# Attention with distance decay: one product per own chunk, pairs of heads unrolled, far chunks finished on VectorE

## The chip, the cores and the metric

The kernel runs on one core of one Trainium2 chip. The metric is the time of one execution on the device in microseconds (us), the median of several runs. Before the change it is 1452.78 us (three runs, 1446.84 to 1455.47).

A core has a matrix engine (TensorE, PE in the profile, with its weight loads as PEld), VectorE (DVE), ScalarE (ACT), GpSimd (POOL) and SyncE (SP), which here issues the transfers. Each runs its own list of instructions in order, and they wait for one another by semaphores. PSUM is the memory that TensorE writes, here eight banks of 128 partitions by 512 fp32 values; SBUF is the main on-chip memory.

## The reference

For x of shape (2, 2048, 256): layer norm, an attention block, layer norm, add to x; then layer norm, a mixture-of-experts block, layer norm, add. The change is in the attention. Cut to that:

```python
q = x @ W_q;  latent = (x @ W_k + x @ W_v) @ W_down_kv
k_rec = latent @ W_up_k;  v_rec = latent @ W_up_v          # 16 heads of 16 columns
scores = einsum('bhqd,bhkd->bhqk', q, k_rec) / sqrt(256)
decay = exp(-0.01 * abs(t[:, None] - t[None, :]))
attn = softmax(scores * decay)                             # the decay multiplies the scores
out = einsum('bhqk,bhkd->bhqd', attn, v_rec) @ W_o
```

## The kernel before

`prologue` normalises x and makes values, queries and keys of the first unit. `attention` then goes over the 32 heads (16 for each batch) in 16 pairs; `layer` does the rest. In `attention` a head is 16 steps, one for each tile of 128 keys (`kt`), and scores lie with keys on partitions and the 2048 queries along the row, in four chunks of 512.

**The decay.** Queries and keys are stored twice, multiplied by a falling and a rising exponential of their place (`FALL`, `RISE`), so that a product of the two gives a decayed score: RISE is right for queries before the key, FALL for those after it. In the 128x128 block where queries and keys are the same places, FALL is used, and VectorE multiplies the block in PSUM by a mask that mends the half above the diagonal (`mask`, L638). The chunk that holds this block is the tile's own chunk. `score_pieces` (L473) cuts it at the block: RISE before, FALL from it on. Where the block isn't at the chunk's start (12 of 16 tiles) that makes two products of the chunk, so a head has 76 score products (L752).

**Halves and the PSUM ring.** A step's scores are made in two halves of 1024 queries (two banks, one product for each bank, on two halves of TensorE's rows). Six banks make a ring of three halves: the scores of a half wait until the exponential of the half three places earlier is done (`exp_done`). ScalarE takes exp of a whole half, PSUM to SBUF (L841), after the mask where the half holds the own block. The products with the values (L764) of step s-2 stand between the two halves of step s on TensorE's list. They sum in the remaining two banks over a head.

**Far chunks.** For the first and the last four key tiles (`FAR_CHUNK`), the query chunk at the other end of the sequence is so far that exp(z) is taken as ((1 + z)^2 + 1) / 2. VectorE reads it from PSUM as 1 + z into the SBUF tile `probs` (`read_far`, L646); GpSimd squares it (L604) and takes half of it plus a half (L607), both in place; ScalarE leaves this chunk out and its exp for this half is 512 wide. The products of the step wait for GpSimd's last pass (`far_sb`).

**Order.** Every head but the very first takes the key tiles in the order `MIXED` = 4, 0, 5, 1, 6, 2, 7, 3, 8, 12, 9, 13, 10, 14, 11, 15: a near tile, a far tile, and so on. Below, N0 and N1 are the first and second half of a near tile, F0 and F1 those of a far tile. The own block of a near tile is in N0, that of a far tile in F1; the far chunk is in F0. So TensorE's list over two steps runs: scores F1, scores N0, products, scores N1, scores F0, products. VectorE's list over the same two steps: `read_far` of F0, mask of F1, mask of N0.

**What stands between.** VectorE copies a head's sums at step 2 (`copy_sums`, L670), TensorE transposes them at step 4 (L771), VectorE divides at step 5 (`normalise`, L675 and L680, after that step's mask). In the first head of 12 pairs, TensorE projects queries and keys of a later unit at steps 7 and 11 (L726) and VectorE prepares them in three pieces each (`prepare`, L657 to L666) at steps 8 to 10 and 12 to 14, after the mask of the step. Below, these are the prep heads (0, 2, ..., 22). Head 0 runs all tiles in their natural order; head 31, the last, leaves out the far treatment and holds work of the next stage.

**The loop.** `pairs` (L530) writes out pair 0, runs pairs 1 to 9 in a hardware loop of three turns with three pairs in its body, and writes out pairs 10 to 15.

Of the kernel before, what the change touches and what calls it, by code (L numbers as in the profile page):

```python
# [10 lines left out]
ALU = mybir.AluOpType  # L11
# [4 lines left out]
P = 128  # L16
# [94 lines left out]
def diagonal_masks(small):  # L111

    return carve(small, 1840, P), carve(small, 1968, P)


# [64 lines left out]
def prologue(nc, io, sem, ident, xT, V_all, decay, small, w_qk, w_unit, K_st, Q_st, work, ps, halves_dram, **_):  # L180
# [39 lines left out]
    with nc.Block() as block:  # L220
        @block.sync
        def _(sp):
# [12 lines left out]
            for r in range(P // STRIP):  # L235
                for sign in range(2):
                    sp.dma_start(decay[STRIP * r:STRIP * (r + 1), sign, :], io["c_decay"][sign]).then_inc(dec_in, 16)
            for mask, dst in enumerate(diagonal_masks(small)):
                sp.dma_start(dst, io["c_diag"][mask]).then_inc(dec_in, 16)
            for n in range(4, NB):  # L240
# [13 lines left out]
            sp.wait_ge(w_in, 6 * 16)  # L254
            sp.wait_ge(dec_in, 10 * 16)
            sp.wait_ge(stack_in, 16 * (4 * QC + 8))
# [30 lines left out]
        def _(dve):  # L287
# [22 lines left out]
            for n in range(NB):  # L310
                dve.wait_ge(x_in[n % 4], 16 * (n // 4 + 1))
                for j in range(CT):
                    i = nc.vector.bn_stats(bn[:, n, j], xin[n % 4][:, j])
                i.then_inc(stats, 1)
                dve.wait_ge(stats, n + 1)
                for j in range(CT):
                    i = nc.vector.bn_aggr(mv[:, n, j], bn[:, n, j])
                i.then_inc(aggr, 1)
                dve.wait_ge(aggr, n + 1)
                nc.vector.tensor_scalar(neg_mean[:, n], mv[:, n, :, 0], -1.0, None, ALU.mult)  # L320
                nc.vector.tensor_scalar(ve[:, n], mv[:, n, :, 1], LN_EPS, None, ALU.add).then_inc(var_eps, 1)
                if n == 1:
                    dve.wait_ge(eff_ps, 1)
                    nc.vector.tensor_copy(w_qk[:, 1], ps[:, 2, :].rearrange("p (k n) -> p k n", k=KD))
                    nc.vector.tensor_copy(w_veff, ps[:, 3, :].rearrange("p (k n) -> p k n", k=KD)).then_inc(eff_sb, 1)
                if n >= 3:
                    if n == 3:
                        dve.wait_ge(dec_in, 10 * 16)
                    prepare(n - 3)
# [102 lines left out]
def attention(nc, sem, ident, xT, V_all, decay, small, w_qk, w_unit, K_st, Q_st, work, ps, attn_dram, halves_dram, first_block, late_keys, **_):  # L432
# [6 lines left out]
    part = carve(work, 13312, 2, 2, 2, CH)  # L439
    dmask, _ = diagonal_masks(small)  # L440
    rden = carve(small, 256, CT, QC)
# [10 lines left out]
    s_.update(att_out=sem("a_att_out"), stk0=sem("a_stk0"), stk1=sem("a_stk1"), out0=sem("a_out0"), out1=sem("a_out1"))  # L452
    bd_all, bd_link, flag, far_link = sem("a_bd_all"), sem("a_bd_link"), sem("a_flag"), sem("a_far_link")
    wait = lambda eng, name, v: eng.wait_ge(s_[name], v + PRIME)
# [10 lines left out]

    def cut(lo, hi):

        while lo < hi:
            end = min(hi, (lo // CH + 1) * CH)
            yield lo, end  # L470
            lo = end

    def score_pieces(kt, half):  # L473

        a, z = half * HALF, (half + 1) * HALF
        own = kt * P
        for lo, hi in cut(a, min(z, own)):
            yield lo, hi - lo, RISE
        for lo, hi in cut(max(a, own), z):
            yield lo, hi - lo, FALL  # L480

# [26 lines left out]
    def half_of(turn, s, k):  # L508

        return 2 * ((turn * NHALF + 2 * s + k) % (ACC // 2))  # L510
# [12 lines left out]

    def own_block(turn, s, kt):

        at = kt * P % HALF
        bank = half_of(turn, s, own_at(kt)) + at // CH
        return ps[:, bank, at % CH:at % CH + P]

    def pairs(eng, pair):  # L530

        pair(0, True, True, False, 0)
        with eng.Fori(1, 1 + 3 * RING, RING) as it:
            for j in range(RING):
                pair(it + j, True, False, False, (1 + j) % RING)
        for it in range(1 + 3 * RING, NPAIR - 1):
            pair(it, it < NPAIR - PPU, False, False, it % RING)
        pair(NPAIR - 1, False, False, True, (NPAIR - 1) % RING)

    with nc.Block() as block:  # L540
# [43 lines left out]
        def _(pool):  # L584
            first_block["gpsimd_start"](pool)
            prime(pool, "vg", "w", "att_out", "stk0", "stk1", "out0", "out1", "far_sq", "far_sb")

# [7 lines left out]

            def far_probs(turn, n, s, order):

                kt = order[s]
                if kt not in FAR_CHUNK:
                    return  # L600
                done = n * NFAR + far_before(order, s) + 1
                p = probs[:, probs_of(turn, s), chunk(FAR_CHUNK[kt])]
                wait(pool, "far_read", done)
                nc.gpsimd.tensor_tensor(p, p, p, ALU.mult).then_inc(s_["far_sq"], 1)  # L604
                wait(pool, "far_sq", done)
                pool.sem_inc(far_link, 1)
                nc.gpsimd.tensor_scalar(p, p, 0.5, 0.5, ALU.mult, ALU.add).then_inc(s_["far_sb"], 1)  # L607

            def pair(it, prep, first, last, third):
                for par in range(2):  # L610
                    n = it * 2 + par
                    turn = 2 * third + par
                    order = NATURAL if first and par == 0 else MIXED
                    if not (last and par):
                        wait(pool, "pv_done", n * NSTEP)
                        values(n + 1, 1 - par)
                        for s in range(NSTEP):
                            if s == 2 and par == 0 and prep:
                                wait(pool, "proj_ps", 2 * it)
                                weights((it // PPU + 1) % KD)  # L620
                            far_probs(turn, n, s, order)
                    else:
# [8 lines left out]
        def _(dve):  # L631
            first_block["vector_start"](dve)
            prime(dve, *"proj_free prep_link prep_sb masked o_sb rden_sb att_sb far_read".split())

            def mask(turn, n, s, kt):

                wait(dve, "sc_ps", n * NHALF + 2 * s + own_at(kt) + 1)
                nc.vector.tensor_tensor(own_block(turn, s, kt), own_block(turn, s, kt), dmask, ALU.mult).then_inc(s_["masked"], 1)  # L638

            def read_far(first, turn, n, s, kt):  # L640

                c = FAR_CHUNK[kt]
                wait(dve, "sc_ps", n * NHALF + 2 * s + 1)
                if not (first and tiles_done(n, s) <= 0):
                    wait(dve, "pv_done", tiles_done(n, s))
                nc.vector.tensor_scalar(probs[:, probs_of(turn, s), chunk(c)], ps[:, half_of(turn, s, 0) + c % 2], SCALE, 1.0,  # L646
                                        ALU.mult, ALU.add).then_inc(s_["far_read"], 1)

            def prepare(piece, c, which, k, bank):
# [39 lines left out]
            def pair(it, prep, first, last, third):  # L689
                for par in range(2):  # L690
                    n = it * 2 + par
                    idle = ACC + 1 - par
                    for s, kt in enumerate(NATURAL if first and par == 0 else MIXED):
                        if kt in FAR_CHUNK and not (last and par):
                            read_far(first, 2 * third + par, n, s, kt)
                        mask(2 * third + par, n, s, kt)
                        if s == 2 and not (first and par == 0):
                            copy_sums(n - 1, 1 - par)
# [21 lines left out]
        def _(pe):  # L720
# [19 lines left out]
            def scores(first, turn, n, s, k, order, far):  # L740
# [5 lines left out]
                if far or 2 * s + k < 3:  # L746
                    far_read(first, n, s, k, order)
                for q0, w, a in score_pieces(kt, half):
                    c = q0 // CH
                    tile = slice(c % 2 * TILE_ROWS, (c % 2 + 1) * TILE_ROWS)  # L750
                    at = c // 2 * CH + q0 % CH
                    m = nc.tensor.matmul(ps[:, half_of(turn, s, k) + c % 2, q0 % CH:q0 % CH + w],  # L752
                                         K_st[tile, par, a, kt * P:(kt + 1) * P], Q_st[tile, par, a, at:at + w], start=True, stop=True)
                m.then_inc(s_["sc_ps"], 1)
# [1794 lines left out]
def constants():  # L2549
# [3 lines left out]
    s, q = np.arange(P)[:, None], np.arange(P)[None, :]  # L2553
    diag = np.where(s > q, np.exp(-2 * DECAY * (s - q)), 1.0)
    pack = lambda v: np.ascontiguousarray(v, dtype=np.float32).view(np.uint32)[:, ::2] >> 16 | np.ascontiguousarray(v, dtype=np.float32).view(np.uint32)[:, 1::2]
    above = s < q
    e = np.arange(NE)
    line = np.concatenate([e, e * S, e * P, np.arange(NT), (e[None, :] <= e[:, None]).reshape(-1)])
    route = np.concatenate([pack(above).view(np.float32), pack(np.ones((P, P))).view(np.float32), np.tile(line, (P, 1)).astype(np.float32)], axis=1)
    out = {"c_ident": np.eye(P), "c_decay": decay, "c_diag": np.stack([diag, diag.T]), "c_route": route, "c_zero": np.zeros((P, D))}  # L2560
    return {k: np.ascontiguousarray(v, dtype=np.float32) for k, v in out.items()}
# [17 lines left out]
```

## Time and profile before

| | |
|---|---|
| median of three runs | 1452.78 us |
| the profiled execution | 1457.08 us |
| its span, first to last instruction | 1453.1 us |
| PE busy | 1307.9 us (90%) |
| ACT busy | 1059.6 us (73%) |
| DVE busy | 711.9 us (49%) |
| POOL busy | 624.5 us (43%) |
| mean granted TensorE clock | 0.956 |

The shares are means over stages with different limits. The 32 heads run from about 86 to about 1086 us of the span. Matrix products are pipelined, and the profile models their ends, so that a busy PE may still be waiting; starts are better to read than busy time.

### The profile page before, as it was taken

Reading aid. Unit: us, or ns where it says so; the run is one execution under the profiler, and the core shown is the slowest. Engines: PE = TensorE matmul, PEld = TensorE weight load, DVE = VectorE, ACT = ScalarE, POOL = GpSimd, SP = SyncE. Lnnn points to the kernel's source line nnn. Section 1 sums busy time; section 2 is a strip of 40 time slices with the busy share of each in tenths; the row PEclk is TensorE's granted clock in tenths of the full one; section 3 lists DMA queues with packets and bytes.
Section 4 is the critical chain, followed back from the end, with each engine's and each line's share of the span. In section 5 each row is a group of like instructions: output and inputs, shape, how many; then the busy total and the mean of one; then the engine's idle time right before and its main releaser. Section 6 shows DMA issues by size and latency. Waiting matters only on the chain. (4 is left out here: it accounts for less than half of the span.)

```text
span 1453.1 us, 27412 instructions
## 1 busy us (share of the span) xinstructions
PE 1307.9 (90%) x8496; PEld 582.6 (40%) x8497; DVE 711.9 (49%) x1948; ACT 1059.6 (73%) x1419; POOL 624.5 (43%) x745
## 2 busy tenths in 40 slices
PE   7879999999999999999999999999987867889881
PEld 4623333333333333333333333333335546657541
DVE  5525535454453535445354443333324566685754
ACT  4558898987989888898988899999953534544532
POOL 2525444443445444444444444444202543333574
PEclk9979999999999999999999999999988987999996
DMA  7775566654566655556665566546962224457843
GB/s 195 252 179 132 136 153 159 128 146 109 134 152 147 158 119 145 124 124 160 143 161 103 145 126 134 105 97 135 244 127 73 91 91 153 160 189 225 248 126 106
DMA packets 141170, 212.00 MB, mean 146 GB/s; under 512 B 56864, under 2 KB 102816, under 8 KB 132768
## 3 DMA queue, kind: packets, MB, share of 16 engines
q1 hardware_dynamic: 134496, 192.86, 53.6%
q0 software_dynamic: 6144, 16.79, 3.6%
q8 instruction: 77, 1.26, 0.4%
q14 instruction: 69, 0.57, 0.1%
q10 hardware_dynamic: 384, 0.52, 0.1%
HBM read 147.19 MB, written 67.11 MB: 147 GB/s over the span
## 5 line engine op out<-in xcount | busy, mean ns | idle before, releaser
L841 ACT ACTIVATE work<-ps 128x1024 f32<-128x1024 f32 (+1 forms) x1024 | 866.0, 928 | 139.4 <-DVE ps L638 109.2
L764 PE MATMUL ps<-work 128*32 128x512 f32 x4096 | 551.4, 611 | 4.3 <-POOL work L607 3.6
L752 PE MATMUL ps<-Q_st,K_st 64*128 64x512 f32 (+3 forms) x2432 | 422.8, 423 | 33.6 <-ACT work L841 14.3
L604 POOL TENSOR_TENSOR work<-work 128x512 f32<-128x512 f32 x248 | 257.9, 1040 | 413.5 <-DVE work L646 413.5
L752 PEld LDWEIGHTS ps<-Q_st,K_st 64*128 64x128 f32 x2432 | 225.0, 185 | 515.8 <-ACT work L841 259.9
L646 DVE TENSOR_SCALAR work<-ps 128x512 f32<-128x512 f32 x248 | 171.2, 690 | 286.5 <-PE ps L752 286.1
L638 DVE TENSOR_TENSOR ps<-ps,small 128x128 f32<-128x128 f32 x512 | 150.6, 298 | 261.7 <-PE ps L752 254.9
L607 POOL TENSOR_SCALAR work<-work 128x512 f32<-128x512 f32 x248 | 154.3, 622 | 49.1 <-POOL work L604 49.1
L764 PEld LDWEIGHTS ps<-work 128*32 128x32 f32 x4096 | 82.1, 108 | 128.5 <-issue 73.5
L2219 POOL DMA_INDIRECT xT<-y_dram,decay x64 | 65.5, 1023 | 62.8 <-DMA xT<-y_dram,decay 27.7
L2201 POOL DMA_INDIRECT xs_dram<-part,decay x64 | 66.5, 1039 | 56.2 <-DMA xs_dram<-part,decay 24.7
L2378 PE MATMUL ps<-stack,work 128*128 x384 | 55.1, 291 | 0.0
L2378 PEld LDWEIGHTS ps<-stack,work 128*128 128x128 f32 x384 | 50.5, 205 | 0.9 <-issue 0.9
L726 PE MATMUL ps<-xT,w_unit 128*128 (+1 forms) x96 | 47.6, 619 | 0.0
L2348 PE MATMUL ps<-decay,work 128*128 128x256 f32 x128 | 34.6, 425 | 11.9 <-DVE work L2427 11.9
L2434 DVE COPY work<-ps 128x512 f32<-128x512 f32 x48 | 33.1, 689 | 23.3 <-PE ps L2360 22.7
L2360 PE MATMUL ps<-ident,work 128*128 128x128 f32 x192 | 32.3, 294 | 12.4 <-DVE work L2434 10.9
L2285 ACT ACTIVATE work<-work,small 128x256 f32<-128x256 f32 x32 | 16.9, 590 | 34.4 <-POOL small L2227 34.3
L2396 PE MATMUL ps<-stack,work 64*128 x96 | 36.5, 463 | 5.1 <-ACT work L2277 4.2
L589 POOL COPY work<-V_all 128x256 f32 (+1 forms) x32 | 12.6, 397 | 63.2 <-PE ps L764 62.4
L2263 ACT ACTIVATE decay<-ps 128x128 f32<-128x128 f32 x48 | 13.2, 276 | 36.2 <-PE ps L2378 36.1
L2272 ACT COPY small<-stack 64x256 f32 x48 | 19.3, 402 | 27.7 <-PE ps L2397 27.3
(184 smaller groups left out, 1149.9 us busy)
## 6 DMA issues: line engine op xcount, KB each, us to landing
K_st<-halves_dram SPq DMA_DIRECT2D x248, 256.0 KB, 5.5
halves_dram<-work SPq DMA_DIRECT2D x64, 512.0 KB, 3.9
Q_st<-halves_dram SPq DMA_DIRECT2D x248, 128.0 KB, 5.8
work<-xs_dram SPq DMA_DIRECT2D x96, 128.0 KB, 2.6
y_dram<-work SPq DMA_DIRECT2D x48, 256.0 KB, 2.8
work<-in_L_attn_x SPq DMA_DIRECT2D x16, 512.0 KB, 7.3
attn_dram<-work SPq DMA_DIRECT2D x16, 256.0 KB, 6.9
work<-attn_dram SPq DMA_DIRECT2D x8, 512.0 KB, 4.5
```

The source lines that it names most:

```text
L604: nc.gpsimd.tensor_tensor(p, p, p, ALU.mult).then_inc(s_["far_sq"], 1)
L607: nc.gpsimd.tensor_scalar(p, p, 0.5, 0.5, ALU.mult, ALU.add).then_inc(s_["far_sb"], 1)
L638: nc.vector.tensor_tensor(own_block(turn, s, kt), own_block(turn, s, kt), dmask, ALU.mult).then_inc(s_["masked"], 1)
L646: nc.vector.tensor_scalar(probs[:, probs_of(turn, s), chunk(c)], ps[:, half_of(turn, s, 0) + c % 2], SCALE, 1.0, ALU.mult, ALU.add).then_i ...
L726: m = nc.tensor.matmul(ps[:, bank], w_unit[:, which, k], xT[:, k, at:at + CH] if isinstance(at, int) else xT[:, k, bass.ds(at, CH)], start ...
L752: m = nc.tensor.matmul(ps[:, half_of(turn, s, k) + c % 2, q0 % CH:q0 % CH + w], K_st[tile, par, a, kt * P:(kt + 1) * P], Q_st[tile, par, a ...
L764: m = nc.tensor.matmul(ps[STRIP * c:STRIP * (c + 1), ACC + par], Vg[:, par, kt], probs[:, probs_of(turn, s), chunk(c)], start=s == 0, stop ...
L841: nc.scalar.activation(probs[:, probs_of(turn, s), chunks[0] * CH:(chunks[-1] + 1) * CH], src, ACT.Exp, scale=SCALE).then_inc(s_["exp_done ...
L2201: nc.gpsimd.indirect_dma_start(xs_dram[r // 4], bass.IndirectOffsetOnAxis(ap=at, axis=0), xn[r % 2][:, j], None).then_inc(put_done[r % 2][ ...
L2219: nc.gpsimd.indirect_dma_start(yg[n % 2][:, j, i], None, y_dram[b], bass.IndirectOffsetOnAxis(ap=at, axis=0)).then_inc(fetched(n, j, i), 16)
L2378: m = nc.tensor.matmul(ps[:, GU[g % 2], at:at + P], xsT[:, g % 2, k, a], w_gu[:, k * NE * P:(k + 1) * NE * P][:, bass.ds(experts[i][a], P) ...
L2396: nc.tensor.matmul(ps[:, DOWN[0], 0:D], hT[0:MR, g % 2], w_dr[0:MR, bass.ds(experts[i][0] * 2, D)], start=True, stop=True)
```

## The change

Four things change in `attention`, and one constant with them.

1. The own chunk is made by one FALL product of 512 queries (`decay_of` takes the place of `score_pieces`): 64 score products a head.
2. VectorE's mask covers all of the own chunk up to the end of its own block, 128, 256, 384 or 512 columns by kt % 4 = 0, 1, 2, 3 (`own_chunk`), and mends the queries before the block as well. The mask is one constant of 128x512 (`c_wide`, 256 KB) in place of two of 128x128.
3. GpSimd's two passes over a far chunk go to VectorE (`finish_far`), after the mask of the same step.
4. All 16 pairs are written out; there is no loop.

```diff
+    def decay_of(kt, c):
+        return FALL if c >= kt // CT else RISE
-    def own_block(turn, s, kt):
-        at = kt * P % HALF
-        bank = half_of(turn, s, own_at(kt)) + at // CH
-        return ps[:, bank, at % CH:at % CH + P]
+    def own_chunk(turn, s, kt):
+        width = (kt % CT + 1) * P
+        return ps[:, half_of(turn, s, own_at(kt)) + kt // CT % 2, 0:width], wide[:, CH - width:]
     def pairs(eng, pair):
-        pair(0, True, True, False, 0)
-        with eng.Fori(1, 1 + 3 * RING, RING) as it:
-            for j in range(RING):
-                pair(it + j, True, False, False, (1 + j) % RING)
-        for it in range(1 + 3 * RING, NPAIR - 1):
-            pair(it, it < NPAIR - PPU, False, False, it % RING)
-        pair(NPAIR - 1, False, False, True, (NPAIR - 1) % RING)
+        for it in range(NPAIR):
+            pair(it, it < NPAIR - PPU, it == 0, it == NPAIR - 1, it % RING)
...
@@ block.gpsimd
-            def far_probs(turn, n, s, order):
...
-                wait(pool, "far_read", done)
-                nc.gpsimd.tensor_tensor(p, p, p, ALU.mult).then_inc(s_["far_sq"], 1)
-                wait(pool, "far_sq", done)
-                pool.sem_inc(far_link, 1)
-                nc.gpsimd.tensor_scalar(p, p, 0.5, 0.5, ALU.mult, ALU.add).then_inc(s_["far_sb"], 1)
...
@@ block.vector
             def mask(turn, n, s, kt):
                 wait(dve, "sc_ps", n * NHALF + 2 * s + own_at(kt) + 1)
-                nc.vector.tensor_tensor(own_block(turn, s, kt), own_block(turn, s, kt), dmask, ALU.mult).then_inc(s_["masked"], 1)
+                own, mended = own_chunk(turn, s, kt)
+                nc.vector.tensor_tensor(own, own, mended, ALU.mult).then_inc(s_["masked"], 1)
+            def finish_far(turn, n, s, order):
+                done = n * NFAR + far_before(order, s) + 1
+                p = probs[:, probs_of(turn, s), chunk(FAR_CHUNK[order[s]])]
+                wait(dve, "far_read", done)
+                nc.vector.tensor_tensor(p, p, p, ALU.mult).then_inc(s_["far_sq"], 1)
+                wait(dve, "far_sq", done)
+                nc.vector.tensor_scalar(p, p, 0.5, 0.5, ALU.mult, ALU.add).then_inc(s_["far_sb"], 1)
...
                         if kt in FAR_CHUNK and not (last and par):
                             read_far(first, 2 * third + par, n, s, kt)
                         mask(2 * third + par, n, s, kt)
+                        if kt in FAR_CHUNK and not (last and par):
+                            finish_far(2 * third + par, n, s, order)
...
@@ block.tensor, scores
-                for q0, w, a in score_pieces(kt, half):
+                for c in (2 * half, 2 * half + 1):
+                    a = decay_of(kt, c)
...
@@ constants
+    before = np.arange(P - CH, P)[None, :]
+    wide = np.where(s > before, np.exp(-2 * DECAY * (s - before)), 1.0)
```

## Rows read from the trace of the kernel before

**Rows 1.** Stretches, one head each: start:end, length, busy us by engine (instructions), clock.

```profile
897.65:926.05 28.40, 28.38 (x210) 9.99 (x208) 11.34 (x28) 26.77 (x32) 13.63 (x18) 1.00 0.60 122
779.05:812.38 33.33, 32.36 (x218) 11.23 (x216) 18.38 (x40) 27.20 (x32) 14.10 (x19) 1.00 0.60 150
655.24:688.69 33.45, 32.38 (x218) 11.16 (x216) 18.69 (x39) 27.18 (x32) 14.02 (x19) 1.00 0.62 154
688.69:717.25 28.56, 28.39 (x210) 9.99 (x208) 11.39 (x28) 26.78 (x32) 13.79 (x18) 1.00 0.58 127
307.81:340.66 32.85, 29.98 (x211) 10.19 (x209) 11.34 (x28) 26.98 (x32) 13.61 (x18) 0.95 0.64 141
```

**Rows 2.** TensorE in order of time, plain steps: start, length, operation, [idle before <-releaser].

```profile
906.93 1.06 PE L764 MATMUL ps<-work 128*32 128x512 f32 x8
...
908.76 1.06 PE L764 MATMUL ps<-work 128*32 128x512 f32 x8
...
910.43 1.07 PE L764 MATMUL ps<-work 128*32 128x512 f32 x8
```

**Rows 3.** VectorE in order of time, the same plain steps.

```profile
907.05 0.69 DVE L646 TENSOR_SCALAR work<-ps 128x512 f32<-128x512 f32 x1 [0.83 <-PE ps L752]
908.48 0.70 DVE L638 TENSOR_TENSOR ps<-ps,small 128x128 f32<-128x128 f32 x2 [0.74 <-PE ps L752]
```

**Rows 4.** VectorE, head 22, steps 13 and 14, with a piece of prepare between two masks.

```profile
804.46 0.30 DVE L638 TENSOR_TENSOR ps<-ps,small 128x128 f32<-128x128 f32 x1 [0.74 <-PE ps L752]
804.67 0.68 DVE L660 TENSOR_REDUCE small<-ps 128x1 f32<-128x512 f32 x1
...
806.19 0.29 DVE L638 TENSOR_TENSOR ps<-ps,small 128x128 f32<-128x128 f32 x1
```

**Rows 5.** ScalarE, then TensorE, behind that late mask.

```profile
806.51 1.02 ACT L841 ACTIVATE work<-ps 128x1024 f32<-128x1024 f32 x1 [0.69 <-DVE ps L638]
...
807.43 1.02 ACT L841 ACTIVATE work<-ps 128x1024 f32<-128x1024 f32 x1
...
808.59 0.50 PE L752 MATMUL ps<-Q_st,K_st 64*128 64x512 f32 x2 [0.51 <-ACT work L841]
809.02 1.07 PE L764 MATMUL ps<-work 128*32 128x512 f32 x8
```

**Rows 6.** Groups by line and shape, VectorE: xcount | busy us, mean ns of one | idle before.

```profile
L638 DVE TENSOR_TENSOR ps<-ps,small 128x128 f32<-128x128 f32 x512 | 150.6, 298 | 261.7 <-PE ps L752 254.9
L680 DVE TENSOR_TENSOR work<-ps,small 128x256 f32<-128x256 f32 x32 | 13.6, 425 | 2.0
L2014 DVE TENSOR_TENSOR decay<-decay 128x512 f32<-128x512 f32 x2 | 1.4, 692 | 0.1
L309 DVE COPY w_qk<-work 128x512 f32<-128x512 f32 x1 | 0.4, 422 | 0.0
L1897 DVE TENSOR_SCALAR part<-part,small 128x256 f32<-128x256 f32 x32 | 11.1, 412 | 6.5 <-POOL small L1862 6.4
```

**Rows 7.** VectorE at step 5 of a head, TensorE at step 4, TensorE at step 7 of a prep head.

```profile
905.09 0.30 DVE L638 TENSOR_TENSOR ps<-ps,small 128x128 f32<-128x128 f32 x1 [0.74 <-PE ps L752]
...
905.92 0.29 DVE L638 TENSOR_TENSOR ps<-ps,small 128x128 f32<-128x128 f32 x1
...
901.11 1.07 PE L764 MATMUL ps<-work 128*32 128x512 f32 x8
...
903.55 0.64 PE L764 MATMUL ps<-work 128*32 128x512 f32 x4
...
788.33 1.07 PE L764 MATMUL ps<-work 128*32 128x512 f32 x8
...
791.68 0.50 PE L752 MATMUL ps<-Q_st,K_st 64*128 64x512 f32 x2
```

**Rows 8.** TensorE at the loop's back edge, in head 7.

```profile
335.30 0.50 PE L752 MATMUL ps<-Q_st,K_st 64*128 64x512 f32 x2 [2.70 <-issue]
335.73 1.51 PE L764 MATMUL ps<-work 128*32 128x512 f32 x8
```

More of the change, by code:

```diff
@@ L113, in diagonal_masks, with wide_mask @@
     return carve(small, 1840, P), carve(small, 1968, P)
+def wide_mask(small):
+    return carve(small, 400, CH)
 def chunk_at(c):
@@ L237, in _ @@
                     sp.dma_start(decay[STRIP * r:STRIP * (r + 1), sign, :], io["c_decay"][sign]).then_inc(dec_in, 16)
-            for mask, dst in enumerate(diagonal_masks(small)):
-                sp.dma_start(dst, io["c_diag"][mask]).then_inc(dec_in, 16)
+            sp.dma_start(wide_mask(small), io["c_wide"]).then_inc(dec_in, 16)
             for n in range(4, NB):
@@ L254, in _ @@
             sp.wait_ge(w_in, 6 * 16)
-            sp.wait_ge(dec_in, 10 * 16)
+            sp.wait_ge(dec_in, 9 * 16)
             sp.wait_ge(stack_in, 16 * (4 * QC + 8))
@@ L327, in _ @@
                     if n == 3:
-                        dve.wait_ge(dec_in, 10 * 16)
+                        dve.wait_ge(dec_in, 9 * 16)
                     prepare(n - 3)
@@ L439, in attention @@
     part = carve(work, 13312, 2, 2, 2, CH)
-    dmask, _ = diagonal_masks(small)
+    wide = wide_mask(small)
     rden = carve(small, 256, CT, QC)
@@ L452, in attention @@
     s_.update(att_out=sem("a_att_out"), stk0=sem("a_stk0"), stk1=sem("a_stk1"), out0=sem("a_out0"), out1=sem("a_out1"))
-    bd_all, bd_link, flag, far_link = sem("a_bd_all"), sem("a_bd_link"), sem("a_flag"), sem("a_far_link")
+    bd_all, bd_link, flag = sem("a_bd_all"), sem("a_bd_link"), sem("a_flag")
     wait = lambda eng, name, v: eng.wait_ge(s_[name], v + PRIME)
@@ L464, in attention @@
     chunk = lambda c: slice(c * CH, (c + 1) * CH)
[L466 to L480, printed above, removed]
+    def decay_of(kt, c):
+        return FALL if c >= kt // CT else RISE
     RING = 3
@@ L585, in _ @@
             first_block["gpsimd_start"](pool)
-            prime(pool, "vg", "w", "att_out", "stk0", "stk1", "out0", "out1", "far_sq", "far_sb")
+            prime(pool, "vg", "w", "att_out", "stk0", "stk1", "out0", "out1")
             def values(m, par):
@@ L594, in _ @@
             values(0, 0)
-            def far_probs(turn, n, s, order):
[L598 to L602, printed above, removed]
-                wait(pool, "far_read", done)
-                nc.gpsimd.tensor_tensor(p, p, p, ALU.mult).then_inc(s_["far_sq"], 1)
-                wait(pool, "far_sq", done)
-                pool.sem_inc(far_link, 1)
-                nc.gpsimd.tensor_scalar(p, p, 0.5, 0.5, ALU.mult, ALU.add).then_inc(s_["far_sb"], 1)
             def pair(it, prep, first, last, third):
@@ L611, in pair @@
                     n = it * 2 + par
-                    turn = 2 * third + par
-                    order = NATURAL if first and par == 0 else MIXED
                     if not (last and par):
@@ L616, in pair @@
                         values(n + 1, 1 - par)
[L617 to L621, printed above, removed]
+                        if par == 0 and prep:
+                            wait(pool, "proj_ps", 2 * it)
+                            weights((it // PPU + 1) % KD)
                     else:
@@ L632, in _ @@
             first_block["vector_start"](dve)
-            prime(dve, *"proj_free prep_link prep_sb masked o_sb rden_sb att_sb far_read".split())
+            prime(dve, *"proj_free prep_link prep_sb masked o_sb rden_sb att_sb far_read far_sq far_sb".split())
             def mask(turn, n, s, kt):
                 wait(dve, "sc_ps", n * NHALF + 2 * s + own_at(kt) + 1)
-                nc.vector.tensor_tensor(own_block(turn, s, kt), own_block(turn, s, kt), dmask, ALU.mult).then_inc(s_["masked"], 1)
+                own, mended = own_chunk(turn, s, kt)
+                nc.vector.tensor_tensor(own, own, mended, ALU.mult).then_inc(s_["masked"], 1)
             def read_far(first, turn, n, s, kt):
@@ L692, in pair @@
                     idle = ACC + 1 - par
-                    for s, kt in enumerate(NATURAL if first and par == 0 else MIXED):
+                    order = NATURAL if first and par == 0 else MIXED
+                    for s, kt in enumerate(order):
                         if kt in FAR_CHUNK and not (last and par):
@@ L747, in scores @@
                     far_read(first, n, s, k, order)
-                for q0, w, a in score_pieces(kt, half):
-                    c = q0 // CH
+                for c in (2 * half, 2 * half + 1):
+                    a = decay_of(kt, c)
                     tile = slice(c % 2 * TILE_ROWS, (c % 2 + 1) * TILE_ROWS)
-                    at = c // 2 * CH + q0 % CH
-                    m = nc.tensor.matmul(ps[:, half_of(turn, s, k) + c % 2, q0 % CH:q0 % CH + w],
-                                         K_st[tile, par, a, kt * P:(kt + 1) * P], Q_st[tile, par, a, at:at + w], start=True, stop=True)
+                    m = nc.tensor.matmul(ps[:, half_of(turn, s, k) + c % 2], K_st[tile, par, a, kt * P:(kt + 1) * P],
+                                         Q_st[tile, par, a, half * CH:(half + 1) * CH], start=True, stop=True)
                 m.then_inc(s_["sc_ps"], 1)
@@ L2559, in constants @@
     route = np.concatenate([pack(above).view(np.float32), pack(np.ones((P, P))).view(np.float32), np.tile(line, (P, 1)).astype(np.float32)], axis=1)
-    out = {"c_ident": np.eye(P), "c_decay": decay, "c_diag": np.stack([diag, diag.T]), "c_route": route, "c_zero": np.zeros((P, D))}
+    out = {"c_ident": np.eye(P), "c_decay": decay, "c_diag": np.stack([diag, diag.T]), "c_wide": wide, "c_route": route, "c_zero": np.zeros((P, D))}
     return {k: np.ascontiguousarray(v, dtype=np.float32) for k, v in out.items()}
```

## The prediction, made before the change ran

> **What bounds the kernel now.** The busy table was read first (PE 90%, ACT 73%, DVE 49%), then a table by heads [rows 1]: a plain head (without prepare) takes 28.40 us at full clock, and in it TensorE has products under way for 28.38. So the stage of the heads is TensorE's by this view, and VectorE looks free for 60% of it (11.34 of 28.40). The order of time says how close the others are. Products start 1.67 us apart where nothing is late (908.76 to 910.43) and 1.83 in the step before [rows 2]; sixteen steps of 1.66 and the turning of sums (2.44 in place of 1.66, so 0.78) [rows 7] would be 27.34 us, so that 1.06 us of a plain head is not TensorE's. In the turn shown, one read of a far chunk and both masks are all that VectorE does, and the masks of F1 and N0 run one behind the other, from 908.48 to 909.18, because the scores of the two halves are neighbours on TensorE's list [rows 3]. What follows if the second of these masks is late, the trace shows too. In head 22 a piece of prepare stands between them: the second starts 1.73 us after the first, not 0.21 (0.30 less the 0.09 by which neighbours on VectorE overlap, 804.46 + 0.30 against 804.67) [rows 4]. ScalarE then idles 0.69, takes the exp of N0 0.03 after the mask, that of N1 0.92 later, and 0.14 after the end of this one (807.43 + 1.02 = 808.45 to 808.59) TensorE, idle for 0.51, begins the scores that had waited for the bank [rows 5]. So a delay of 1.52 between these two masks is hidden by 0.83 and shows by 0.69. Both numbers are used below.
>
> **The change, part by part.**
>
> *The far passes.* On VectorE's list they stand just there: read of F0, mask of F1, square, half plus a half, mask of N0. The square is an fp32 TENSOR_TENSOR of 128x512 in SBUF: 0.69 (L2014). For the other pass, one tensor in and immediates, there are two bounds: 0.42, a copy of 128x512 in SBUF (L309), and 0.69, the same operation and shape read from PSUM [rows 3] and what 256 columns in 0.412 (L1897) make for 512 columns [rows 6]. I take 0.42: the copy has the same traffic, one row in and one out, while L1897 also reads two scalars for each partition. The upper end is a rival below. The wait between the passes is put at the 0.03 that ScalarE needs behind VectorE. With two overlaps of 0.09 the passes add 0.69 + 0.03 + 0.42 - 0.09 = 1.05 behind the mask of F1, itself overlapped by 0.09: 0.96 in all.
>
> The Trainium skill ("VectorE: DVE Perf Modes", section "The perf-mode tier table") has fp32 tensor_copy and tensor_scalar between SBUF tiles at two elements a cycle and tensor_tensor at one. L309 and L2014 agree with it; L1897, a tensor_scalar of 256 columns in 0.412 us, doesn't. By the rule the sum is the forecast below, by L1897 it is the first rival.
>
> *The wide masks.* 128 columns take 0.30 (L638), 256 from PSUM 0.43 (L680), 512 take 0.69; 384 lie between, 0.56 [rows 6, 3]. A pair of masks (F1, N0) is then 0.73, 1.00, 1.25 or 0.99 in place of 0.60, on average 0.99.
>
> *The lap.* From the start of N0's scores: products 0.43 later (808.59 to 809.02), the next products 1.66 later, the mask of the next F1 1.55 behind them (906.93 to 908.48), then the mask of F1 (m1), 0.96 for the passes, the mask of N0 (m2), 0.03, 0.92 to the exp of N1, 1.02 for it, and 0.14 to the scores that wait for its banks [rows 2 to 5]. These are the scores of N0 two turns (four steps) after the first ones. Sum: 5.75 + 0.96 + m1 + m2, on average 7.70 us for two turns, so 3.85 a turn, where TensorE alone needs 2 x 1.66 = 3.32 and the head of before takes (28.40 - 0.78) / 8 = 3.45. Two such laps run interleaved; a head is four of each, and the slower sets the pace. VectorE as such would fit: 0.69 + 0.96 + 0.99 in 3.85. It is the order of its list that costs.
>
> *A plain head.* The slower lap has the transposes (0.78) and normalise, which stands between the last pass and the next mask at step 5 (905.09 to 905.92, 0.83 less 0.21 = 0.62) [rows 7]. Its four pairs of masks sum to 0.73 + 1.25 + 0.73 + 1.25 = 3.96. So 4 x 6.71 + 3.96 + 0.78 + 0.62 = 32.2 us, 3.8 more than 28.40. There are 19 (the odd heads to 23, then 24 to 30): 72 us. copy_sums at step 2 stands behind the second mask and ahead of a read with room; nothing.
>
> *A prep head* takes 33.33 [rows 1]. First lap 5.75 + 0.96 + 0.73 = 7.44. In the second the projection holds TensorE (its scores start 3.35 behind the products, 788.33 to 791.68) [rows 7]: 0.43 + 1.66 + 0.78 + 1.34 to the N0 between, then 0.43 + 1.66 + 3.35, so 9.65, more than VectorE's lap of 9.36. Third and fourth have prepare's second piece between the masks, now behind the passes: 7.44 + 1.52 and 7.96 + 1.52. Sum 35.5, 2.2 more; heads 2 to 22, 11 of them: 24 us.
>
> *Heads 0 and 31.* Head 0 has its far tiles one behind the other, eight times 0.96 and wider masks on a list that is partly full: between 0 and 8 x 1.35 = 11, I take 5. Head 31 has no passes, only wider masks: between 0 and 16 x 0.39 = 6, I take 1.
>
> *One product in place of two.* Its gain is a part of the 1.06 us that a plain head has above TensorE's own. In the lap above every score half is two products, so the gain is in the sum already, and what TensorE wins is time in which it waits.
>
> *Unrolling.* A back edge stops TensorE for 2.70 us, and the steps behind it are slow [rows 8]: heads with one take 32.85 against 28.56. That is 4.3 us, twice. In the loop a prep head takes 33.45 against 33.33 and another 28.56 against 28.40 [rows 1]; I count 0.2 for each of nine pairs. Together 10.5 us less. That written-out code costs nothing elsewhere is read from heads 20 to 30, which are written out already; the bound on the other side is one stop of 4.3 for each further pair, 9 x 4.3 = 39, which nothing there shows.
>
> *Nothing:* the larger constant is loaded once ahead of the heads. GpSimd keeps only its copies of values and weights, which now start earlier; no queue of transfers is moved. `far_sb` comes sooner than from GpSimd, and the products that wait for it stand a step later on TensorE's list.
>
> *Sum.* 72 + 24 + 5 + 1 - 10.5 = +92. On the profiled execution's 1457.1 that is 1549, and as the median of before lies 4.3 lower, 1545.
>
> **The rivals.**
>
> *The last pass at the slow rate* (0.69): 0.27 more in each of four laps of 30 heads, 32 us: 1577. For it L1897, against it L309.
>
> *The clock falls.* TensorE now idles about 0.5 us a turn. Behind the 2.70 of the back edge products took 1.51 in place of 1.06 [rows 8]; behind an idle time of 0.51 they took 1.07 [rows 5], and that head was at clock 1.00 [rows 1]. One such fall a head at 1.6 us (335.73 on, half of what the back edge costs beyond its stop) would be about 48: near 1600.
>
> *Half hidden.* By the other way to count, from what head 22 hid: passes and wider masks put 0.96 + 0.39 = 1.35 between the masks, 0.83 is hidden, 0.52 shows in a lap, which would then be 6.90 + 0.52 = 7.42 and not 7.70. The 0.28 between are the slower starts of a TensorE that was idle (the 0.14 and 0.43 of the lap). If most of them are caught up elsewhere, 4 x 0.28 x 30 = 34 goes: 1511.
>
> *Faster.* The mechanism: the mask of N0 still ends before ScalarE has come to it, so that the passes lie in VectorE's idle time, and TensorE sets the pace with fewer products. It decides for itself if passes and wider masks add less than the 0.83 that was hidden in head 22. By the rows they add 1.35. For it speaks VectorE's 60% idle. Then 10.5 go by unrolling and, of 1.06 in each of 31 heads, say half, 16: 1426.
>
> **How the numbers follow.** Forecast 0.47, with a range of its own from 1520 to 1570; slow pass 0.25; clock 0.05; half hidden 0.15; faster 0.06; and 0.02 that gains and losses cancel. The range from 1500 to 1590 leaves out the faster cases, the clock and the ends of the others, 0.2 in all. A difference of 0.5% (7 us) is what a measurement of this kernel can tell from none. Faster 0.06, same 0.02, slower 0.92.
>
> **What would show it.** Right: plain heads near 32 us, regular; ScalarE waiting for VectorE's mask (L638's successor) in most turns; masks of N0 that start 1.3 to 1.7 behind the start of the masks of F1; TensorE idle 0.4 to 0.6 before the scores of N0; no stop in heads 7 and 13. The square at 0.69 and the last pass at 0.42 or 0.69 decide between the forecast and the first rival. Wrong: heads of 28 us or less with masks that wait for scores, not for VectorE, or TensorE at half clock.

## The result, and the profile after

The changed kernel takes 1571.99 us (median of four runs, 1570.29 to 1574.16) against 1454.12 for the kernel before on the same chip: a ratio of 1.0817, 95% interval 1.0771 to 1.0864. It is slower by 118 us; 1545 was forecast, in a range from 1500 to 1590 (the forecast's own range ended at 1570), and the sign, the place and the chain were as predicted. One term, the prep heads, was too small.

Groups of VectorE by line and shape, kernel after (xcount | busy us, mean ns | idle before, who ended it). They answer to [rows 6]: the square takes the 0.69 of L2014, the last pass the 0.42 of L309, and the four widths of the mask lie on the line that was drawn.

```profile
L624 DVE TENSOR_TENSOR work<-work 128x512 f32<-128x512 f32 x248 | 171.4, 691 | 0.0
L626 DVE TENSOR_SCALAR work<-work 128x512 f32<-128x512 f32 x248 | 105.8, 427 | 8.6
L608 DVE TENSOR_TENSOR ps<-ps,small 128x512 f32<-128x512 f32 x128 | 88.9, 695 | 51.7 <-PE ps L733 51.7
L608 DVE TENSOR_TENSOR ps<-ps,small 128x384 f32<-128x384 f32 x128 | 72.0, 562 | 59.4 <-PE ps L733 59.4
L608 DVE TENSOR_TENSOR ps<-ps,small 128x256 f32<-128x256 f32 x128 | 54.8, 428 | 40.0 <-PE ps L733 39.8
L608 DVE TENSOR_TENSOR ps<-ps,small 128x128 f32<-128x128 f32 x128 | 37.9, 296 | 63.8 <-PE ps L733 63.7
```

The last pass is a tensor_scalar with immediates between SBUF tiles: here the rule of the Trainium skill ("VectorE: DVE Perf Modes", "The perf-mode tier table") holds, with 0.427 us against the 0.691 of the tensor_tensor of the same shape, and L1897 of [rows 6], with a scalar for each partition, was no guide.

Now one turn of a plain head in order of time, VectorE, then ScalarE, then TensorE (start, length, [idle before <- who ended it]). It answers to [rows 2, 3].

```profile
1024.17 0.43 DVE L608 TENSOR_TENSOR ps<-ps,small 128x256 f32<-128x256 f32 x1 [0.73 <-PE ps L733]
1024.51 0.68 DVE L624 TENSOR_TENSOR work<-work 128x512 f32<-128x512 f32 x1
1025.23 0.43 DVE L626 TENSOR_SCALAR work<-work 128x512 f32<-128x512 f32 x1
1025.57 0.56 DVE L608 TENSOR_TENSOR ps<-ps,small 128x384 f32<-128x384 f32 x1
1026.49 0.69 DVE L616 TENSOR_SCALAR work<-ps 128x512 f32<-128x512 f32 x1 [0.36 <-PE ps L733]
```

```profile
1026.16 1.94 ACT L822 ACTIVATE work<-ps 128x1024 f32<-128x1024 f32 x2 [0.50 <-DVE ps L608]
```

```profile
1027.37 0.49 PE L733 MATMUL ps<-Q_st,K_st 64*128 64x512 f32 x2
1028.15 0.50 PE L733 MATMUL ps<-Q_st,K_st 64*128 64x512 f32 x2 [0.29 <-ACT work L822]
1028.58 0.64 PE L745 MATMUL ps<-work 128*32 128x512 f32 x4
```

The masks of F1 and N0 start 1.40 us apart with the two passes between them. ScalarE idles 0.50 and takes the exp of N0 0.03 after the mask (1025.57 + 0.56 = 1026.13 to 1026.16); its two exps end at 1028.10, TensorE begins the waiting scores at 1028.15, and its products 0.43 later. Over the span ScalarE waits 227.0 us for the mask (before 109.2).

By heads, kernel after (start:end, length, busy us of PE, PEld, DVE, ACT, POOL with their instructions, clock, DMA share, GB/s). They answer to [rows 1]: a plain head, a prep head at full clock, a prep head in which the clock falls, and the stretch where it does.

```profile
1004.28:1036.20 31.92, 29.43 (x199) 8.40 (x197) 21.90 (x44) 27.12 (x33) 0.40 (x1) 1.00 0.52 108
232.17:270.00 37.83, 33.14 (x207) 9.76 (x205) 29.24 (x56) 27.37 (x32) 0.65 (x2) 1.00 0.53 135
301.92:341.02 39.10, 34.42 (x206) 9.97 (x205) 29.02 (x55) 27.48 (x33) 0.65 (x2) 0.96 0.52 127
334.00:341.00 7.00, 5.72 (x28) 1.59 (x28) 4.03 (x8) 5.61 (x7) 0.40 (x1) 0.76 0.49 169
```

Added up over the profiled executions (1453.1 and 1569.4 us, from the first product with the values of a head to that of the next):

| | before | after | difference | forecast |
|---|---|---|---|---|
| head 0 | 35.9 | 40.1 | +4.2 | +5 |
| 12 odd heads, 1 to 23, loop costs in them | 351.0 | 384.6 | +33.6 | +36 |
| 11 prep heads, 2 to 22, loop costs in them | 368.0 | 427.7 | +59.7 | +23 |
| heads 24 to 30 | 198.8 | 223.5 | +24.7 | +27 |
| head 31, and all outside the heads | 499.4 | 493.5 | -5.9 | +1 |
| span | 1453.1 | 1569.4 | +116.3 | +92 |

The forecast of a row is its heads times the gain of one, less the loop's share. The heads lie where they were forecast, to 3 us a row, but for the prep heads. Of the row of head 31 and all outside little can be read: in the profiled executions of the other kernels here it runs from 488.7 to 498.0, whichever engine does the far passes.

### The profile page after: what moved, and what is told of

Same layout as the page of the kernel before. It is cut to its first block and busy times, and to the rows that moved or that the text cites. A ratio compares the mean times of both kernels' runs of the same rounds, so it can differ in the third digit from the quotient of the medians.

```text
span 1569.4 us, 23832 instructions
## 1 busy us (share of the span) xinstructions
PE 1340.7 (85%) x8112; PEld 531.9 (34%) x8113; DVE 1040.8 (66%) x2444; ACT 1068.9 (68%) x1419; POOL 212.9 (14%) x249
## 5 line engine op out<-in xcount | busy, mean ns | idle before, releaser
L822 ACT ACTIVATE work<-ps 128x1024 f32<-128x1024 f32 (+1 forms) x1024 | 875.3, 924 | 251.5 <-DVE ps L608 227.0
L733 PE MATMUL ps<-Q_st,K_st 64*128 64x512 f32 x2048 | 453.9, 479 | 121.8 <-ACT work L822 102.2
L733 PEld LDWEIGHTS ps<-Q_st,K_st 64*128 64x128 f32 x2048 | 178.5, 187 | 655.6 <-ACT work L822 504.8
L608 DVE TENSOR_TENSOR ps<-ps,small 128x256 f32<-128x256 f32 (+3 forms) x512 | 253.6, 495 | 214.9 <-PE ps L733 214.6
L624 DVE TENSOR_TENSOR work<-work 128x512 f32<-128x512 f32 x248 | 171.4, 691 | 0.0
L575 POOL COPY work<-V_all 128x256 f32<-128x256 f32 x32 | 12.8, 401 | 1028.9 <-PE ps L745 1028.3
L626 DVE TENSOR_SCALAR work<-work 128x512 f32<-128x512 f32 x248 | 105.8, 427 | 8.6
L708 PE MATMUL ps<-xT,w_unit 128*128 128x512 f32 x96 | 47.6, 618 | 0.0
L2329 PE MATMUL ps<-decay,work 128*128 128x256 f32 x128 | 33.0, 410 | 10.7 <-DVE work L2408 10.7
L2311 PE MATMUL ps<-xT,w_qk 128*128 128x512 f32 x64 | 33.9, 656 | 6.1 <-DVE work L2408 5.1
L2266 ACT ACTIVATE work<-work,small 128x256 f32<-128x256 f32 x32 | 16.9, 590 | 31.3 <-POOL small L2208 31.2
```

Of the source, the lines that this page charges most:

```text
L608: nc.vector.tensor_tensor(own, own, mended, ALU.mult).then_inc(s_["masked"], 1)
L624: nc.vector.tensor_tensor(p, p, p, ALU.mult).then_inc(s_["far_sq"], 1)
L626: nc.vector.tensor_scalar(p, p, 0.5, 0.5, ALU.mult, ALU.add).then_inc(s_["far_sb"], 1)
L708: m = nc.tensor.matmul(ps[:, bank], w_unit[:, which, k], xT[:, k, at:at + CH] if isinstance(at, int) else xT[:, k, bass.ds(at, CH)], start ...
L733: m = nc.tensor.matmul(ps[:, half_of(turn, s, k) + c % 2], K_st[tile, par, a, kt * P:(kt + 1) * P], Q_st[tile, par, a, half * CH:(half + 1 ...
L822: nc.scalar.activation(probs[:, probs_of(turn, s), chunks[0] * CH:(chunks[-1] + 1) * CH], src, ACT.Exp, scale=SCALE).then_inc(s_["exp_done ...
```

## The experiments

Ratios are to the kernel before on the same chip, with 95% intervals. A plain head is one of 24 to 30 in the profile.

**Both passes behind the next mask.** In the changed kernel:

```diff
                         mask(2 * third + par, n, s, kt)
-                        if kt in FAR_CHUNK and not (last and par):
-                            finish_far(2 * third + par, n, s, order)
+                        if s and order[s - 1] in FAR_CHUNK and not (last and par):
+                            finish_far(2 * third + par, n, s - 1, order)
+                        if s == NSTEP - 1 and kt in FAR_CHUNK and not (last and par):
+                            finish_far(2 * third + par, n, s, order)
```

> The changed kernel, with the square and the last pass of a far chunk moved on VectorE's list behind the mask of the next step (7 of 8 times in a head; the far tile of step 15 keeps its place). VectorE does the same work. Theory (the passes cost because they stand ahead of the mask of N0): that mask starts again right behind the mask of F1, a plain head falls from 31.93 to 28.6 to 29.4 us, prep heads by 2 to 3 us, the kernel to 1480 to 1500 us. Rival (the amount of VectorE's work sets the pace): no more than 10 us below 1572.

Measured: 1550.15 us, 1.066 (1.0616 to 1.0704); plain heads 31.20 us. Neither theory: 22 us of the gain, not 80. The order of time says why. VectorE and TensorE of this run:

```profile
1012.69 1.17 DVE L608 TENSOR_TENSOR ps<-ps,small 128x384 f32<-128x384 f32 x2 [0.86 <-PE ps L735]
1013.77 0.68 DVE L624 TENSOR_TENSOR work<-work 128x512 f32<-128x512 f32 x1
1014.48 0.43 DVE L626 TENSOR_SCALAR work<-work 128x512 f32<-128x512 f32 x1
```

```profile
1012.87 1.06 PE L747 MATMUL ps<-work 128*32 128x512 f32 x8
1015.06 1.06 PE L747 MATMUL ps<-work 128*32 128x512 f32 x8 [0.19 <-DVE work L626]
```

The masks now follow each other, and the products wait for the last pass, which ends at 1014.91. In the plain head 28 the products of five of the eight far tiles start 0.14 or 0.15 behind the end of their last pass, so that this chain holds most turns. The place behind both masks is too late for the products of the same tile, which come one turn after its scores. A theory on the place has to name both ends; mine had named one.

**The passes back on GpSimd**, all else as changed.

> The changed kernel with GpSimd's two passes back where they were; the wide masks, the single products and the written-out pairs stay. Theory: the far passes are the whole loss; what is left is 10.5 us of unrolling and the wide masks. A lap through the exp of F1 is 6.5 us plus the mask of F1, now 0.43 to 0.56 on average in place of 0.30, so that a plain head is 28.4 to 28.9 us and the kernel 1443 to 1460. Rival (the single products win what they leave out): plain heads of 27.4 to 28.0 us, 1415 to 1432.

Measured: 1471.98 us, 1.0129 (1.0096 to 1.0162); a plain head 29.46, a prep head 34.08. So the passes are 100 of the 118 us in the changed kernel, and what stays is more than expected: slower than before even with the loop gone.

**Unrolling alone.** `pairs` writes out all 16 pairs, nothing else.

> The kernel before with all pairs written out, nothing else. Theory: two back edges of 4.3 us and 0.2 us for each of nine pairs go, 10.5 us: 1443 to 1444. Rival (written-out code has to be fetched and stalls once or more for a pair): no gain or a loss, 1454 to 1490.

Measured: 1439.71 us, 0.991 (0.9879 to 0.9941). Gain 13.5 us, 3 more than expected, with 10.5 inside the interval; in the profiled executions heads 0 to 30 give 10.6 and the rest lies outside them. Heads 7 and 13 take 28.48 like their neighbours, and no stop came in elsewhere. Against this kernel, the single products and wide masks of the run before it cost 32 us: a plain head 29.48 against 28.40 (means of heads 24 to 30).

**The passes alone**, in the kernel before with loop, cut chunks and masks of 128 columns.

> The kernel before with the far passes on VectorE, with the loop, the cut chunks and the masks of 128 columns. Theory: a lap is 5.75 + 0.96 + 0.60 = 7.31 us, a plain head 4 x 7.31 + 1.40 = 30.6, prep heads 1.3 to 1.6 us under those of the changed kernel, loop costs as before: 1535 to 1548. Rival (the wide masks are the larger part of the loss): under 1500.

Measured: 1540.81 us, 1.0615 (1.0575 to 1.0654); plain heads 30.36 us, 0.24 under the lap's 30.6. The total and the plain heads are as expected. Two things beside them aren't: ten of the 11 prep heads fell in clock (37.8 to 38.2 us at a granted clock of 0.95 or 0.96, the one at full clock 36.72), and the heads with a back edge are 5.5 and 5.8 us longer than their neighbours, not 4.3.

**The square ahead of the mask of F1, the last pass behind the mask of N0**, in the changed kernel (`square_far` is the first half of `finish_far`):

```diff
                             read_far(first, 2 * third + par, n, s, kt)
+                            square_far(2 * third + par, n, s, order)
                         mask(2 * third + par, n, s, kt)
-                        if kt in FAR_CHUNK and not (last and par):
-                            finish_far(2 * third + par, n, s, order)
+                        if s and order[s - 1] in FAR_CHUNK and not (last and par):
+                            finish_far(2 * third + par, n, s - 1, order)
...
```

> The changed kernel with the same passes on VectorE in other places: the square ahead of the mask of F1, behind the read (VectorE is idle there), and the last pass behind the mask of the next step (again but for step 15). In the run with both passes behind the next mask the products had waited for the last pass (1014.91 to 1015.06), which is a chain of its own: 1.55 to the mask of F1, both masks and both passes, 0.14, about 3.6 us a turn. Theory (it is the place on the list): here that chain is 0.69 shorter and the masks follow each other, so plain heads come to those with GpSimd's passes, 29.3 to 29.9 us, and the kernel to 1478 to 1505. Rival (the amount of work on VectorE): no better than the run with both passes behind the mask, 1540 or more.

Measured: 1496.78 us, 1.0305 (1.0273 to 1.0337); plain heads 29.65, 0.17 above what GpSimd's passes gave. VectorE does the same instructions as in the changed kernel, 75 us faster. The 25 us by which it is still behind the run with GpSimd's passes are for the most part in the prep heads (35.6 against 34.1 us) and in head 0 (42.1 against 36.9).

**The same places with the cut chunks**, in the written-out kernel before.

> The written-out kernel before, cut chunks and masks of 128 columns, with the far passes on VectorE: the square ahead of the mask of F1, the last pass behind the mask of the next step. Theory (the place): the passes are hidden, plain heads 28.4 to 28.9 us, prep heads up to 1.5 us above those with GpSimd, the kernel 1440 to 1465. Rival (the amount): plain heads above 29.5, the kernel above 1490.

Measured: 1446.83 us, 0.9967 (0.9946 to 0.9989). VectorE, and two heads of this run:

```profile
934.63 0.69 DVE L626 TENSOR_SCALAR work<-ps 128x512 f32<-128x512 f32 x1 [0.51 <-PE ps L751]
935.36 0.69 DVE L633 TENSOR_TENSOR work<-work 128x512 f32<-128x512 f32 x1
936.06 0.71 DVE L618 TENSOR_TENSOR ps<-ps,small 128x128 f32<-128x128 f32 x2
936.67 0.42 DVE L640 TENSOR_SCALAR work<-work 128x512 f32<-128x512 f32 x1
```

```profile
925.25:953.62 28.37, 28.37 (x211) 10.02 (x209) 19.44 (x44) 26.77 (x32) 0.64 (x2) 1.00 0.51 110
217.79:251.75 33.96, 32.84 (x218) 11.38 (x216) 26.16 (x56) 27.43 (x33) 1.21 (x3) 1.00 0.63 156
```

The square fills the time from the read to the mask of F1, which starts on the heel of it, and a plain head takes what it takes with GpSimd, 28.37 against 28.40, with VectorE busy for 19.44 us in place of 11.38. The passes cost nothing there; in prep heads 0.6 us, and in head 0, with far tiles in a row, 2.8.

**One product and the wide mask for near tiles only**, in the written-out kernel before.

```diff
     def score_pieces(kt, half):
+        if kt not in FAR_CHUNK:
+            for c in (2 * half, 2 * half + 1):
+                yield c * CH, CH, FALL if c >= kt // CT else RISE
+            return
...
```

> The written-out kernel before (far passes on GpSimd) with one product and the wide mask for the own chunks of near tiles only; far tiles are cut as before, with the mask of 128 columns. Theory (the wide mask costs by the mask of F1, which is on the lap F1, N0, N1; that of N0 has 0.55 us of room): plain heads 28.1 to 28.5, the kernel 1432 to 1446. Rival (both masks cost alike): plain heads near 28.9, the kernel near 1456.

Measured: 1450.57 us, 1.0007 (0.9985 to 1.0029), 11 us slower than without; a plain head 28.70. My range was missed by 4.6 us, and both halves are to blame: of the 1.08 us that single products with wide masks add to a plain head, those of near tiles make 0.30 here, which leaves some 0.8 to those of far tiles (by subtraction; they weren't tried alone). Nowhere does a product less make a head shorter; but no run has the single products without the wide masks, so that a gain below the masks' cost isn't ruled out.

**The projection ahead of the waiting scores**, in the changed kernel: the calls of `project` at steps 7 and 11 stand ahead of `scores(first, turn, n, s, 1, ...)`.

> The changed kernel with the projections of steps 7 and 11 ahead of the scores of that step's second half on TensorE's list, not behind them. Theory (in the changed kernel the projection stands behind scores that wait for the exp of N0, so its 1.93 us are added to the wait): the two long steps of a prep head go from 4.63 and 5.13 to 3.8 to 4.3 us, a prep head from 37.8 to 39.2 to 36 to 37.2, the kernel to 1540 to 1555; plain heads stay at 31.9. Rival (the prep heads' excess is VectorE's work in them): the steps only shift, the kernel at 1565 or more.

Measured: 1541.88 us, 1.0621 (1.0591 to 1.0652). Heads of this run, a prep head and a plain one:

```profile
225.49:261.96 36.47, 33.36 (x206) 9.75 (x204) 28.94 (x56) 27.24 (x33) 0.66 (x2) 1.00 0.56 140
1005.24:1037.18 31.94, 29.45 (x198) 8.39 (x196) 21.88 (x44) 27.13 (x33) 0.40 (x1) 1.00 0.45 98
```

The 11 prep heads sum to 401.1 us in place of 427.7, all at full clock, with VectorE as busy as before; plain heads stand. So the rival is out. But the order is not the whole excess: a prep head at full clock gets 1.36 us shorter, from 37.83, and 35.5 was forecast. The two long steps went to 3.57 and 3.58, below what was expected, while steps beside them grew (in head 4 four steps of 1.66 became 2.12, 2.18, 1.86 and 2.44).

**Without the square**, in the changed kernel (the far scores are not squared).

> The changed kernel without the square of the far chunks (so that the far scores are left out of the square; one pass of 0.69 us and one wait less between the two masks). Theory: a lap is 5.75 + 0.33 + 0.99 us, a plain head 29.5 to 30.0 us, near the 29.47 that the wide masks alone gave, and the kernel 1490 to 1505. Rival (a turn is set by something else than that stretch between the masks): plain heads stay above 31.

Measured (one run): 1482.41 us; plain heads 29.73 us, as the lap had it. The total is 8 us under the expected range: prep heads fall to 34.75 at full clock.

**A version that beats both.** In the written-out kernel before, prepare's reduction goes ahead of the mask of F1 and the rest of that piece behind the mask of N0:

```diff
...
+                        if prep and par == 0 and s in (9, 13):
+                            prepare(1, it % PPU, s // 13, 2 * it + s // 13, idle)
                         mask(2 * third + par, n, s, kt)
...
-                        if prep and par == 0 and s >= 8 and s < 11:
+                        if prep and par == 0 and s in (8, 10):
                             prepare(s - 8, it % PPU, 0, 2 * it, idle)
-                        if prep and par == 0 and s >= 12 and s < 15:
+                        if prep and par == 0 and s in (12, 14):
                             prepare(s - 12, it % PPU, 1, 2 * it + 1, idle)
```

> The written-out kernel before (cut chunks, GpSimd's passes) with prepare's second piece parted: its reduction goes ahead of the mask of F1 (steps 9 and 13), where VectorE is idle, the rest behind the mask of N0 (steps 10 and 14), with the third piece. Nothing of it stands between the two masks then. Theory (what stands between these masks is what costs): the steps of 4.13 and 2.72 us in the prep heads go to 3.77 and 1.8 or so, prep heads from 33.36 to 32.0 to 32.4 us, the kernel to 1424 to 1433, below the written-out kernel's 1440. Rival (VectorE is simply full in these steps): no change, 1437 to 1443.

Measured: 1423.74 us, 0.9812 (0.978 to 0.9844), the fastest here. A prep head, as [rows 1] have it at 33.33 and the unrolled kernel at 33.36:

```profile
212.11:244.36 32.25, 32.25 (x218) 11.24 (x216) 18.89 (x40) 27.20 (x32) 15.08 (x19) 1.00 0.63 156
```

## Why the prediction was right, and which term was too small

**The lap.** Plain heads came at 31.92 us, 32.2 forecast, and its links are seen one by one in the turn above. One of them was read too long: from the end of N1's exp to the scores, 0.14 in the forecast, it is 0.05 there (1028.10 to 1028.15). So the half-hidden rival, by which slow starts of TensorE would be caught up, has a small part: 0.07 of its 0.28 a lap. The signs came, but for one: in the head from 1004.28 on TensorE idles ahead of the scores of N0 in five of eight turns, for 0.16 to 0.50 us, where 0.4 to 0.6 was named. That the stretch between the masks of F1 and N0 is what costs was tested from both sides: taking 0.69 and a wait out of it (no square) took 2.2 us from a plain head; taking both passes out of it without less work brought the heads from 31.92 to 29.65 and, with narrow masks, from 30.36 to 28.37, though only to 31.20 where the passes then held the products; taking prepare's piece out of it made the kernel before faster, too.

**The widths and the last pass** had the forecast's values. The rival with the slow last pass (0.69) is out: 0.427. The total near that rival's 1577 has another cause, and that it lies in the stated range at all is in part luck: the room above 1570 had been left for the slow pass, which didn't come, and the prep heads filled it.

**Prep heads: the step that failed**, as the prediction put it: in the second lap the projection "holds TensorE" at 3.35 behind the products, and the third has no term for it at all and no reason why not. But on TensorE's list the projection stands behind the scores of F1, and these wait for the exp of N0 of the turn before, which is late itself. The 1.9 us come after that wait, not beside it. TensorE of the kernel after, steps 7 and 11 of head 4; where [rows 7] had 3.35 from products to scores, it is 4.20 and 4.70:

```profile
242.30 1.07 PE L745 MATMUL ps<-work 128*32 128x512 f32 x8
244.16 0.50 PE L733 MATMUL ps<-Q_st,K_st 64*128 64x512 f32 x2 [0.79 <-ACT work L822]
244.59 1.99 PE L708 MATMUL ps<-xT,w_unit 128*128 128x512 f32 x4
246.50 0.50 PE L733 MATMUL ps<-Q_st,K_st 64*128 64x512 f32 x2
...
251.97 1.06 PE L745 MATMUL ps<-work 128*32 128x512 f32 x8
254.33 0.49 PE L733 MATMUL ps<-Q_st,K_st 64*128 64x512 f32 x2 [1.30 <-ACT work L822]
254.75 1.98 PE L708 MATMUL ps<-xT,w_unit 128*128 128x512 f32 x4
256.67 0.50 PE L733 MATMUL ps<-Q_st,K_st 64*128 64x512 f32 x2
```

A prep head at full clock takes 37.83, not 35.5: 11 x 2.3 = 25 us. The miss lies in just these two laps. Every fourth step, products of head 4 start at 236.22, 246.93, 257.10 and 266.47 us, which makes laps of 10.7, 10.2 and 9.4 us where 9.65, 8.96 and 9.48 were forecast; the other four steps of the head take 7.6 against 7.44. With the projection first a prep head takes 36.47, and its second lap is 9.66, as forecast; the third is still 9.5. So 1.36 of the 2.33 us is the place of the projection, and for the other 1.0 the cause stays open.

**The clock**, a rival given 0.05, came in part: 8 of the 11 prep heads take 39.1 to 40.3 us. TensorE, behind the late mask of step 14 of head 6:

```profile
334.78 0.51 PE L733 MATMUL ps<-Q_st,K_st 64*128 64x512 f32 x2 [1.56 <-ACT work L822]
335.79 0.60 PE L733 MATMUL ps<-Q_st,K_st 64*128 64x512 f32 x2 [0.50 <-ACT work L822]
336.31 1.93 PE L745 MATMUL ps<-work 128*32 128x512 f32 x8
338.18 1.22 PE L733 MATMUL ps<-Q_st,K_st 64*128 64x512 f32 x4
```

After idle times of 1.56 and 0.50 us TensorE runs for some 3 us at 1.2 GHz (the granted clock of the 7 us from 334.00 is 0.76, products take 1.93 in place of 1.06). Over the 8 heads that is 11.6 us. The price of one fall, 1.6, was nearly right (1.3 to 2.4); the prediction had weighed it on plain heads, and all of these are at a granted clock of 1.00. Both together, 25 and 12, are the 37 us by which the prep heads miss; of the 12 us fewer elsewhere, 7 are in the row of head 31 and all outside.

**Unrolling** was sized right (10.5 against 13.5, interval about 9 to 18). **Single products**: with their masks they gain nothing, as forecast; alone they weren't tried. The wide masks are 0.39 in the lap, 1.56 in the four laps of a plain head, and that was right: from the run with the passes alone (30.36) to the changed kernel (31.92) it is 1.56. With GpSimd's passes, where the forecast lap does not bind, they still cost 1.08 us a plain head. The lap over the exp of F1 that was worked out for that run gave up to 0.5. Over heads 24 to 30 ScalarE waits for masks 42 times, 16.9 us, where the unrolled kernel has 18 times and 7.6 us; that is 1.3 us more a head, so the masks are where it shows, but which chain makes up the rest is open.

## What to carry to other kernels

A half-idle engine has room only at certain places of its list. Before work is moved to it, find the instruction on its list that another engine waits for, and the latest consumer of the moved work, and put it between two places with slack; here the same two passes cost 88 us in one place and 7 in another with masks of 128 columns (against the kernel before and its unrolled form), and 100 and 25 with the wide ones. And what is queued behind a wait on TensorE (here a projection) starts with that wait: put independent work ahead of it.

## What was not expected of the hardware

The same two idle times of TensorE, 1.56 and then 0.50 or 0.51 us, were followed by a fall of its clock in head 6 (products of 1.93 above) and by full clock in head 4:

```profile
265.03 0.50 PE L733 MATMUL ps<-Q_st,K_st 64*128 64x512 f32 x2 [1.56 <-ACT work L822]
266.04 0.50 PE L733 MATMUL ps<-Q_st,K_st 64*128 64x512 f32 x2 [0.51 <-ACT work L822]
266.47 1.07 PE L745 MATMUL ps<-work 128*32 128x512 f32 x8
```

In the run with the projection first no prep head shows a fall. Why one head fell and another did not, no run here shows.
